# Sums by destination over spans of 64 nodes for 128 in a two-layer graph network

## The chip, the cores and the metric

One core of one Trainium2 chip runs the whole network. The metric is device time in microseconds, from start to end of one execution. Lower is better.

## The reference

There are 6250 nodes with 128 features (`x`), 206250 edges sorted by destination (`dst`), each with a source (`src`), a weight and 128 attributes. Both layers sum over edges:

```python
edge_index = jnp.stack([src, dst]); edge_index_t = jnp.stack([src, dst], axis=1)
h = jnp.maximum(_layernorm(x), 0.0)
# layer 0: (row, col) = (src, dst), with a loop of weight 1 at each node
deg = segment_sum(w, row); dinv = rsqrt(deg)
x = x + relu(segment_sum((dinv[row] * w * dinv[col])[:, None] * (h @ kernel)[col], row) + bias)
h = jnp.maximum(_layernorm(x), 0.0)
# layer 1: heads = src, tails = dst, E = edge attributes
msg_fwd  = concatenate([h[heads], E]) @ W_fwd + b_fwd
msg_back = concatenate([h[tails], E]) @ W_back + b_back
agg = segment_sum(concatenate([msg_fwd, msg_back]), concatenate([tails, heads])) / (cnt + 1e-7)
x = x + layernorm(leaky_relu(agg) + h) * gamma + beta
```

The weights are applied after the sums, since both are linear. So what has to be summed are rows of `g = dinv * h` by source, and edge attributes by source and by destination.

## The kernel before

**Groups.** The edges are cut into 202 groups of 1024 (8 for each of 128 partitions, `J = 8`). Since they are sorted by destination, a group touches few neighbouring nodes. `base_i[g]` holds the first destination of group `g`, and an edge's offset is its destination less that. The setup (`setup_and_degrees`) writes the offsets to DRAM (`dst_offset`), keeps them in the group's record (`rec`), and checks that every offset lies within the span that the sums by destination can hold (L449 to L453). If one does not, the flag `dense` is 0 and a general path with a scatter for every row runs in place of `first_layer` and `dense_sums`.

**What is done with a group.** Both stages that the change touches go through groups in the same way.
- VectorE compares the keys of the sources (L851, L1709; eight a group, each 128 x 128) to find edges of one source; TensorE multiplies with the result, so that each source's sum stands in one row (L966 and L967, or L1814).
- ScalarE copies those sums out of PSUM (L1039, L1895), and GpSimd adds them to tables in DRAM with indirect transfers, called scatters here, eight a group (L813, L1643).
- `spot_sums` (VectorE, L827 and L1687) compares the offsets of the 1024 edges with 0 to 127. The result, `sum_hot`, is 128 x 8 x 128. TensorE multiplies the attributes with it into one bank, `win_bank` (L962, L1812; eight products a group, the first three together at chunk 2), and `add_window` (L836, L1696) adds the 128 columns to `attr_sums` at `base`.
- In the first layer only: the rows of `g` that belong to the destinations are loaded (`window`, 128 rows from `base`, L791), the offsets are loaded to all partitions (`rel_b`, L783) and compared with each partition's number (L856, `spread_hot`), and TensorE spreads the rows to the edges (L949). ScalarE weighs them (L1032, `pay`).

**The stages.** `first_layer` takes groups 0 to 107, beside products for the other part of the graph (13 pairs of node tiles, L988, L998). `dense_sums` takes the other 94, most of them in steps beside the 25 tiles of a dense product by counts of edges (L1743, L1744, L1794, L1850, L1870), the last 88 in the first 22 tiles, four a tile.

**Order.** Every engine has a fixed program, and semaphores tie them. At a group's start VectorE runs, in this order, `spot_sums` of this group (after all products of the last), `add_window` of the last group, and then `prepare` for the next group with its eight L851 or L1709, with L856 behind the third. TensorE needs both of the first two at chunk 2:

```python
if j == 2:
    at_least(pe, window_added, g)
    pe.wait_ge(sum_ready, g + 1)
for jj in (range(3) if j == 2 else range(j, j + 1) if j > 2 else ()):
    nc.tensor.matmul(win_bank[:, 0:P], attrs[:, h, jj, :], sum_hot[:, jj, :], start=(jj == 0), stop=(jj == J - 1))
```

A scatter waits for ScalarE's copy and for the landing of the last scatter into its table; ScalarE's copy waits for the landing of the scatter that read its buffer before. SyncE loads in the order offsets, keys, record (after `sum_ready`, L785 and L1581), rows of `g`, attributes (after TensorE's products).

## Time and profile before

| | before |
|---|---|
| median of 3 runs | 4395.79 us (4393.73 to 4401.21) |
| the profiled execution | 4403.89 us |
| its span | 4402.1 us |
| TensorE, weight loads | 3390.4 us, 2833.3 us |
| VectorE | 3169.3 us |
| ScalarE | 1843.2 us |
| GpSimd | 3040.5 us |
| scatters of the first layer (L813) | 493 to 2235 us, 864 of them |
| scatters of the second stage (L1643) | 2444 to 4087 us, 752 of them |

Names in rows: PE is TensorE's matmuls, PEld its weight loads, DVE VectorE, ACT ScalarE, POOL GpSimd, SPq SyncE's queue. A row of a group of instructions reads: line, engine, operation, output<-inputs, shapes, count | busy us, mean ns of one | idle us of the engine just before them, and what ended that. Tiles of the first layer begin with `fl_`, those of the second stage with `ds_`; `shared` is a memory that several tiles of the second stage use, among them `same`, `sum_hot` and the sums. An fp32 matmul is two records.

### The profile page before, as it was taken

The page shows a single profiled execution, that of the slowest core. Times are in us where ns is not written, and L with a number is a line of the kernel's source. Part 1 is how long each engine was busy: PE and PEld are TensorE (multiplying, and loading weights), DVE is VectorE, ACT ScalarE, POOL GpSimd, SP SyncE. Part 2 cuts the span into 40 slices and gives each one's busy share as a digit, 9 for nine tenths or more (in the row PEclk, how much of TensorE's full clock was granted, in tenths as well). Part 3 has the DMA queues.
Part 4 walks back from the last instruction along what each step waited for, and adds up shares of the span by engine and source line. Part 5 has one row for each costly group of instructions (what it writes and reads, how often), then busy time and mean ns, then how long its engine had stood idle before and what let it go on. Part 6 is the DMA issues. An engine that isn't in the chain of part 4 may idle for free. (4 is left out here: it accounts for less than half of the span.)

```text
span 4402.1 us, 100368 instructions
## 1 busy us (share of the span) xinstructions
PE 3390.4 (77%) x30529; PEld 2833.3 (64%) x30529; DVE 3169.3 (72%) x8051; ACT 1843.2 (42%) x4498; POOL 3040.5 (69%) x1812
## 2 busy tenths in 40 slices
PE   1454599888889888889803499889888898889945
PEld 1344587777777777777703377767767677777635
DVE  6999888888888888878614776666666666666427
ACT  1021355545555555555404144444444444444513
POOL 2666488888888888888820688778777777777210
PEclk9989899999999999999956599999999999999977
DMA  9991587777777777777786555455445555554861
GB/s 162 279 217 16 128 142 140 139 140 135 135 141 139 141 136 135 137 135 141 129 131 120 105 84 85 75 78 82 77 77 78 84 77 80 77 83 72 97 124 30
DMA packets 682054, 504.19 MB, mean 115 GB/s; under 512 B 308854, under 2 KB 593920, under 8 KB 679754
## 3 DMA queue, kind: packets, MB, share of 16 engines
q0 software_dynamic: 260032, 176.60, 36.6%
q1 hardware_dynamic: 421475, 320.75, 29.9%
q8 instruction: 288, 4.72, 0.4%
q14 instruction: 259, 2.12, 0.2%
HBM read 283.43 MB, written 240.12 MB: 119 GB/s over the span
## 5 line engine op out<-in xcount | busy, mean ns | idle before, releaser
L1643 POOL DMA_INDIRECT gcn_sums<-shared,ds_to_i x752 | 1309.1, 1741 | 542.5 <-ACT shared L1895 327.6
L813 POOL DMA_INDIRECT gcn_sums<-fl_sums,fl_to_i x864 | 1459.3, 1689 | 290.9 <-DMA gcn_sums<-fl_sums,fl_to_i 151.9
L1850 PE MATMUL bank<-ds_counts,ds_parts 128*128 128x256 bf16 x3675 | 605.5, 278 | 0.0
L1039 ACT COPY fl_sums<-bank 128x256 f32<-128x256 f32 x864 | 324.7, 376 | 641.8 <-DMA gcn_sums<-fl_sums,fl_to_i 303.6
L1919 ACT COPY ds_turned<-bank 128x1024 bf16<-128x1024 bf16 (+1 forms) x325 | 313.1, 963 | 613.4 <-PE bank L1835 520.7
L1883 ACT CAST ds_counts<-bank 128x392 bf16<-128x392 f32 x800 | 382.9, 490 | 225.9 <-PE bank L1794 206.4
L1870 PE MATMUL bank<-ds_turned,ds_now 128*128 128x512 bf16 (+1 forms) x1950 | 463.7, 375 | 0.0
L851 DVE SCALAR_TENSOR_TENSOR fl_same<-fl_key_b,fl_pat,from_me 128x128 f32<-128x128 bf16 x864 | 375.5, 447 | 117.0 <-PE bank L967 93.1
L1779 DVE TENSOR_TENSOR src_sums<-src_sums,bank 128x512 f32<-128x512 f32 (+1 forms) x325 | 213.2, 656 | 278.8 <-PE bank L1870 274.2
L966 PE MATMUL bank<-fl_pay,fl_same 128*128 128x128 f32 x1728 | 350.9, 285 | 66.7 <-issue 38.1
L1812 PE MATMUL bank<-shared 128*128 128x128 f32 x1504 | 306.8, 308 | 115.1 <-DVE attr_sums L1696 87.1
L1709 DVE SCALAR_TENSOR_TENSOR shared<-shared,ds_pat,from_me 128x128 f32<-128x128 bf16 x752 | 312.3, 443 | 106.7 <-PE bank L1814 91.8
L962 PEld LDWEIGHTS bank<-fl_sum_hot,fl_attrs 128*128 128x128 f32 x1728 | 263.8, 192 | 183.4 <-issue 114.0
L1814 PE MATMUL bank<-shared 128*128 128x128 f32 x1504 | 319.2, 296 | 72.6 <-DMA shared<-in_edge_attr 48.7
L962 PE MATMUL bank<-fl_sum_hot,fl_attrs 128*128 128x128 f32 x1728 | 324.1, 290 | 56.0 <-DVE attr_sums L836 54.5
L1850 PEld LDWEIGHTS bank<-ds_counts,ds_parts 128*128 128x128 bf16 x3675 | 344.2, 100 | 32.6
L966 PEld LDWEIGHTS bank<-fl_pay,fl_same 128*128 128x128 f32 x1728 | 272.6, 195 | 113.9 <-issue 99.7
L998 PE MATMUL bank<-fl_hi_w,fl_lo_hot 128*128 128x98 bf16 x4992 | 289.1, 208 | 67.5 <-DVE fl_hi_w L890 61.6
L967 PE MATMUL bank<-fl_attrs,fl_same 128*128 128x128 f32 x1728 | 339.7, 279 | 0.0
L988 PE MATMUL bank<-fl_turned,fl_g_tile 128*128 128x512 f32 (+1 forms) x676 | 332.8, 574 | 3.6 <-DVE gcn_t L899 1.0
L585 PE MATMUL bank<-col_w,row_hot 128*128 128x200 bf16 x1616 | 174.1, 266 | 194.0 <-DVE col_w L507 188.5
L890 DVE TENSOR_TENSOR fl_hi_w<-fl_hi_hot,fl_twos 128x784 bf16<-128x784 bf16 x624 | 317.2, 565 | 8.7
(254 smaller groups left out, 7101.6 us busy)
## 6 DMA issues: line engine op xcount, KB each, us to landing
fl_attrs<-in_edge_attr SPq DMA_DIRECT2D x108, 512.0 KB
shared<-in_edge_attr SPq DMA_DIRECT2D x186, 256.0 KB
fl_rel_b<-dst_offset SPq DMA_DIRECT2D x108, 256.0 KB
fl_key_b<-src_key SPq DMA_DIRECT2D x108, 256.0 KB
gcn_sums<-zeros SPq DMA_DIRECT2D x40, 640.0 KB
shared<-src_key SPq DMA_DIRECT2D x94, 256.0 KB
gcn_sums<-fl_sums,fl_to_i POOLq DMA_INDIRECT x864
near<-src_float SPq DMA_DIRECT2D x1, 12892.0 KB
```

What stands on the lines that cost most here:

```text
L813: nc.gpsimd.indirect_dma_start(out=d.tab_gcn[j % K], out_offset=bass.IndirectOffsetOnAxis(ap=to_i[:, (GPI * kk + gi) % 4, j:j + 1], axis=0 ...
L851: nc.vector.scalar_tensor_tensor(same[:, j, :], key_p[:, h, :, j], pat_f[:, j:j + 1], d.from_me[:], ALU.is_equal, ALU.mult, accum_out=late ...
L962: nc.tensor.matmul(win_bank[:, 0:P], attrs[:, h, jj, :], sum_hot[:, jj, :], start=(jj == 0), stop=(jj == J - 1))
L966: nc.tensor.matmul(sum_bank[j % 2][:, 0:F], same[:, j, :], pay[:, j // U, j % U, :], start=True, stop=True)
L967: nc.tensor.matmul(sum_bank[j % 2][:, F:2 * F], same[:, j, :], attrs[:, h, j, :], start=True, stop=True).then_inc(summed, 1)
L988: nc.tensor.matmul(prod_bank[:, 0:n], g_tile[:, old, :], turned[:, (old + b) % 2, 0:n], start=True, stop=True).then_inc(prod_ready, 1)
L1039: nc.scalar.copy(sums[:, h, j, :], sum_bank[j % 2][:, 0:2 * F]).then_inc(staged, 1)
L1643: nc.gpsimd.indirect_dma_start(out=d.tab_gcn[j % K].rearrange("n (two f) -> (n two) f", two=2), out_offset=bass.IndirectOffsetOnAxis(ap=to ...
L1814: nc.tensor.matmul(sum_bank[:, j % U * F:(j % U + 1) * F], same[:, j, :], attrs[:, half, j % U, :], start=True, stop=True).then_inc(chunk_ ...
L1850: ins = nc.tensor.matmul(row_bank[:, 0:2 * P], parts[:, tile, s, :], counts[:, h, tile, :, :].rearrange("p b q -> p (b q)"), start=(tile = ...
L1870: ins = nc.tensor.matmul(back_bank[v][:, 0:n], now[:, h, half, s, :], turned[:, v, half, 0:n], start=(half == 0 and s == 0), stop=(half == ...
L1883: nc.scalar.copy(to, pair_bank[batch % B][:, 0:PB * HH].rearrange("p (c k) -> p k c", c=PB)).then_inc(pair_copied, 1)
```

## The change

The span falls from 128 to 64 nodes wherever destinations are summed or spread. `W = 64` is new. The setup's bound goes to 64, so a group with an offset of 64 or more would send the whole execution to the general path.

```diff
+W = 64
...
-                nc.vector.tensor_scalar(wide[:, 0:1], wide[:, 0:1], P - 0.5, None, ALU.is_gt)
+                nc.vector.tensor_scalar(wide[:, 0:1], wide[:, 0:1], W - 0.5, None, ALU.is_gt)
...
-        rel_b = sb("rel_b", [P, 2, P, J], BF16)
-        window = sb("window", [P, 2, F])
+        rel_b = sb("rel_b", [W, 2, P, J], BF16)
+        window = sb("window", [W, 2, F])
...
-        spread_hot = sb("spread_hot", [P, J, P])
+        spread_hot = sb("spread_hot", [W, J, P])
...
-        sum_hot = sb("sum_hot", [P, J, P])
+        sum_hot = sb("sum_hot", [P, J, W])
...
-                    sp.dma_start(flat(rel_b[:, h, :, :]), everywhere(d.dst_offset, g)).then_inc(rel_in[h], 16)
+                    sp.dma_start(flat(rel_b[:, h, :, :]), everywhere(d.dst_offset, g, W)).then_inc(rel_in[h], 16)
...
-                    sp.dma_start(window[:, h, :], d.g[bass.ds(base, P), :]).then_inc(window_in[h], 16)
+                    sp.dma_start(window[:, h, :], d.g[bass.ds(base, W), :]).then_inc(window_in[h], 16)
...
-                nc.vector.tensor_tensor(sum_hot[:], d.iota[:].unsqueeze(1).to_broadcast([P, J, P]), rec[:, h, 2, :].unsqueeze(2).to_broadcast([P, J, P]),
+                nc.vector.tensor_tensor(sum_hot[:], d.iota[:, 0:W].unsqueeze(1).to_broadcast([P, J, W]), rec[:, h, 2, :].unsqueeze(2).to_broadcast([P, J, W]),
                                         ALU.is_equal).then_inc(sum_ready, 1)
...
-                at = bass.ds(base, P)
-                nc.vector.tensor_tensor(d.attr_sums[:, at], d.attr_sums[:, at], win_bank[:, 0:P], ALU.add).then_inc(window_added, 1)
+                at = bass.ds(base, W)
+                nc.vector.tensor_tensor(d.attr_sums[:, at], d.attr_sums[:, at], win_bank[:, 0:W], ALU.add).then_inc(window_added, 1)
...
-                    nc.vector.tensor_scalar(spread_hot[:], rel_b[:, h, :, :].rearrange("p q j -> p j q"), d.part[:, 0:1], None,
+                    nc.vector.tensor_scalar(spread_hot[:], rel_b[:, h, :, :].rearrange("p q j -> p j q"), d.part[0:W, 0:1], None,
...
-                    nc.tensor.matmul(win_bank[:, 0:P], attrs[:, h, jj, :], sum_hot[:, jj, :], start=(jj == 0), stop=(jj == J - 1))
+                    nc.tensor.matmul(win_bank[:, 0:W], attrs[:, h, jj, :], sum_hot[:, jj, :], start=(jj == 0), stop=(jj == J - 1))
```

The second stage (`dense_sums`) gets the same edits in `sum_hot`, `spot_sums`, `add_window` and the product at L1812. It has no `rel_b` and no `window`.

## Rows read from the trace of the kernel before

**Rows 1.** The page, busy time of engines over the span.
```profile
PE 3390.4 (77%) x30529; PEld 2833.3 (64%) x30529; DVE 3169.3 (72%) x8051; ACT 1843.2 (42%) x4498; POOL 3040.5 (69%) x1812
```
**Rows 2.** Busy time in two stretches: PE, PEld, DVE, ACT, POOL (instructions), PE clock, DMA share, GB/s.
```profile
1000.00:1200.00 200.00, 174.74 (x1599) 150.53 (x1598) 164.60 (x468) 101.80 (x287) 167.74 (x99) 0.98 0.78 139
3200.00:3400.00 200.00, 174.34 (x1580) 138.28 (x1577) 128.14 (x343) 86.12 (x150) 154.32 (x89) 0.94 0.50 77
```
**Rows 3.** Groups by line on GpSimd, 600 to 2150 us and 2605 to 3940 us.
```profile
L813 POOL DMA_INDIRECT gcn_sums<-fl_sums,fl_to_i x767 | 1299.9, 1695 | 252.5 <-DMA gcn_sums<-fl_sums,fl_to_i 133.7 <-issue 104.3 <-ACT fl_sums L1039 14.5
...
L1643 POOL DMA_INDIRECT gcn_sums<-shared,ds_to_i x612 | 1060.9, 1733 | 276.1 <-issue 157.8 <-ACT shared L1895 105.8 <-DMA gcn_sums<-shared,ds_to_i 12.5
```
**Rows 4.** The page, groups of the scatters over the span.
```profile
L1643 POOL DMA_INDIRECT gcn_sums<-shared,ds_to_i x752 | 1309.1, 1741 | 542.5 <-ACT shared L1895 327.6
L813 POOL DMA_INDIRECT gcn_sums<-fl_sums,fl_to_i x864 | 1459.3, 1689 | 290.9 <-DMA gcn_sums<-fl_sums,fl_to_i 151.9
```
**Rows 5.** The lines of the scatters: duration in ns min/median/max, first and last start.
```profile
L813 POOL DMA_INDIRECT gcn_sums<-fl_sums,fl_to_i x864: 1557/1561/2632, 493.0 to 2233.8; - x173
...
L1643 POOL DMA_INDIRECT gcn_sums<-shared,ds_to_i x752: 1557/1561/2819, 2443.6 to 4085.4; - x188
```
**Rows 6.** Timeline about 1004 us, VectorE and GpSimd: start us, us, instruction.
```profile
1003.90 1.16 DVE L856 TENSOR_SCALAR fl_spread_hot<-fl_rel_b,part 128x1024 f32<-128x1024 bf16 x1
...
1004.09 2.41 POOL L813 DMA_INDIRECT gcn_sums<-fl_sums,fl_to_i  x1 [0.30 <-issue]
```
**Rows 7.** Timelines: first and last held scatter beside L827, then beside L1687.
```profile
518.96 1.22 DVE L827 TENSOR_TENSOR fl_sum_hot<-iota,fl_rec 128x1024 f32<-128x1024 f32 x1
...
519.16 2.46 POOL L813 DMA_INDIRECT gcn_sums<-fl_sums,fl_to_i  x1 [0.30 <-DMA gcn_sums<-fl_sums,fl_to_i]
...
2146.10 1.23 DVE L827 TENSOR_TENSOR fl_sum_hot<-iota,fl_rec 128x1024 f32<-128x1024 f32 x1
...
2146.66 2.10 POOL L813 DMA_INDIRECT gcn_sums<-fl_sums,fl_to_i  x1 [0.30 <-DMA gcn_sums<-fl_sums,fl_to_i]
...
2479.66 1.22 DVE L1687 TENSOR_TENSOR shared<-iota,ds_rec 128x1024 f32<-128x1024 f32 x1
...
2480.60 1.72 POOL L1643 DMA_INDIRECT gcn_sums<-shared,ds_to_i  x1 [0.30 <-issue]
...
4062.71 1.22 DVE L1687 TENSOR_TENSOR shared<-iota,ds_rec 128x1024 f32<-128x1024 f32 x1
...
4063.64 1.72 POOL L1643 DMA_INDIRECT gcn_sums<-shared,ds_to_i  x1 [0.30 <-issue]
```
**Rows 8.** Groups by line and form on VectorE, over the span.
```profile
L827 DVE TENSOR_TENSOR fl_sum_hot<-iota,fl_rec 128x1024 f32<-128x1024 f32 x108 | 131.7, 1220 | 57.0 <-issue 42.1 <-PE bank L967 12.2 <-DVE fl_to_i L864 2.4
...
L1696 DVE TENSOR_TENSOR attr_sums<-attr_sums,bank 128x128 f32 x94 | 26.4, 281 | 0.4 <-issue 0.4
...
L1678 DVE TENSOR_TENSOR src_sums<-src_sums,ds_parts 128x1280 f32<-128x1280 f32 x5 | 7.5, 1493 | 0.2
```
**Rows 9.** Timelines of a tile's start, 2934 to 2946 us: VectorE, TensorE, GpSimd.
```profile
2934.49 1.23 DVE L1743 TENSOR_TENSOR ds_lo_hot<-ds_numbers,ds_twos 128x2048 bf16<-128x2048 bf16 x1
...
2937.66 0.28 DVE L1696 TENSOR_TENSOR attr_sums<-attr_sums,bank 128x128 f32 x1
...
2937.99 0.94 PE L1812 MATMUL bank<-shared 128*128 128x128 f32 x6 [2.39 <-DVE attr_sums L1696]
2938.76 0.39 PE L1814 MATMUL bank<-shared 128*128 128x128 f32 x2
...
2945.03 1.56 POOL L1643 DMA_INDIRECT gcn_sums<-shared,ds_to_i  x1 [2.13 <-ACT shared L1895]
```
**Rows 10.** Waits of TensorE, 600 to 2150 and 2605 to 3940 us: total us, times, longest.
```profile
PE bank L962 <- DVE attr_sums L836: 50.6, 84, 2.0
...
PE bank L1812 <- DVE attr_sums L1696: 46.8, 23, 2.6
```
**Rows 11.** Timeline of TensorE about 279 us: fp32 matmuls with few moving columns.
```profile
278.97 0.42 PE L555 MATMUL bank<-start,ahead 128*128 128x50 f32 x2 [0.62 <-DVE start L423]
279.23 0.39 PE L556 MATMUL bank<-start,wrap 128*128 128x49 f32 x2
```

More of the change, by code:

```diff
@@ L1811, in sum_chunk @@
                 for jj in (range(3) if j == 2 else range(j, j + 1) if j > 2 else ()):
[L1812 removed]
+                    nc.tensor.matmul(win_bank[:, 0:W], attrs[:, jj // U, jj % U, :], sum_hot[:, jj, :], start=(jj == 0), stop=(jj == J - 1))
                 pe.wait_ge(same_ready, ch + 1)
```

13 lines of the change are left out of this document (6 added, 7 removed).

## The prediction

> **What bounds the kernel now.** Read the page first, for which engines are full: TensorE is busy for 77% of the span, GpSimd for 69%, and no engine is full by that figure [rows 1]. The share is an average, so the stretches come next. Two of 200 us, one in each stage that the change touches, show GpSimd at 168 and 154 us with 99 and 89 instructions, TensorE at about 174 us in both, VectorE at 165 and 128 us [rows 2]. GpSimd only issues scatters there, and its busy time leaves out what passes between two of them. The groups by line give that: in 600 to 2150 us 767 scatters take 1299.9 us with 252.5 us idle before them, or 0.33 us each; in 2605 to 3940 us 612 take 1060.9 with 276.1 idle [rows 3]. Before nearly every scatter the idle time is 0.30 us, which is the least that shows anywhere and so the cost of going from one to the next. 1299.9 + 252.5 is 1552 of 1550 us: **in the first layer GpSimd is never without work**. There 767 x 0.305 = 234 of the idle us is that floor, and 18.6 us is a wait for something. In the second stage it is 276.1 - 612 x 0.305 = 89 us, nearly all of it for ScalarE's copy of the sums (105.8 us with its floors): GpSimd sets the pace between hiccups, and TensorE causes those.
>
> The last thing to see is a scatter's own time. The median is 1.561 us in both stages, the mean 1.689 and 1.741, the longest 2.6 and 2.8 [rows 4, 5]. So (1.689 - 1.561) x 864 = 111 us and (1.741 - 1.561) x 752 = 135 us are spent in scatters that are longer than the rest. Where that comes from shows when the timelines of GpSimd and VectorE are laid side by side: a scatter that starts during a long VectorE instruction ends 1.43 us after **that instruction's** end. The one at 1004.09 lasts 2.41 us, to 1006.50; VectorE's comparison for the spread (L856) ran from 1003.90 to 1005.06 [rows 6]. The comparison for the sums (L827, L1687) does the same: 518.96 + 1.22 = 520.18, and the scatter of 519.16 ends at 521.62, 1.44 later; 2479.66 + 1.22 = 2480.88, and that of 2480.60 ends at 2482.32, 1.44 later [rows 7]. A scatter so held costs what is left of VectorE's instruction less 0.13 us. Additions that read PSUM (L899, L1779, L836) hold none in the timeline.
>
> **The change, part by part.**
>
> The comparison for the sums goes from 1024 to 512 elements per partition. VectorE's one with both inputs in SBUF takes 1.220 us for 1024 and 1.493 us for 1280, which is 1.07 ns an element [rows 8]; 512 fewer take 0.546 us off, and leave **0.674 us**. Over 108 + 94 groups that is 110 us of VectorE, which by itself is worth nothing: VectorE has 35 and 72 of 200 us free [rows 2]. It counts in two ways.
>
> *Holds.* If a scatter's start falls anywhere, an instruction of length L holds on average (L - 0.13)^2 / 2T, with T the spacing of scatters, 2.02 us in the first layer and 2.2 in the second stage (200 us by 99 and 89 [rows 2]). Before: 1.09^2 / 4.04 = 0.29 us a group, after: 0.544^2 / 4.04 = 0.073; times 108 is 24 us gained. In the second stage 1.19 / 4.4 - 0.296 / 4.4 = 0.203, times 94 is 19 us. Together 43 us. The other way is to count. I find 32 held scatters at L827, 19.7 us in all, and 71 at L1687, 39.3 us in all (first and last of each in [rows 7]); with each hold shortened by 0.546 us and the starts as they are, 4.3 and 10.8 us stay, which gains 15 + 28.5 = 44 us. Both ways agree in the sum and I take **43 us**. All of it is on the path in the first layer, and in the second stage wherever GpSimd sets the pace. Bounds: nothing (the holds pass on to the next instruction), and 59 us (all of them gone).
>
> *The wait at a tile's start.* Once per tile of the second stage TensorE waits 2.4 us for the addition of the last window (L1696), which stands on VectorE behind three long comparisons: L1743 from 2934.49, L1744, L1687, and the addition at 2937.66; TensorE goes on at 2937.99, and GpSimd then stands idle for 2.13 us before 2945.03 [rows 9]. In that window there are 23 such waits, 46.8 us [rows 10]. The chain gets 0.55 us shorter by L1687 and 0.07 us by the addition (0.281 us for 128 columns, 1.06 ns each by the same slope [rows 8]). Over 21 tiles that is **13 us**; from 0, if the idle time is filled from elsewhere, to 2 x 13 where a tile has a second such gap. In the first layer the same wait is 0.6 us once a group (84 of them, 50.6 us [rows 10]), and it goes altogether, but GpSimd has work all the while: nothing.
>
> *The window's products* (L962, L1812) get 64 moving columns for 128. I cost this at **nothing**, and this is the choice that matters most on TensorE. Each fp32 product is two records, and each loads 128 x 128 weights. The only fp32 products with few moving columns are at 278.97 us: two of 50 and two of 49 columns. The pairs last 0.42 and 0.39 us, as long as a pair with 128 columns (0.39, at 2938.76 [rows 9]), and the second pair starts 0.26 us behind the first, so one record takes some 0.11 to 0.13 us whatever it moves [rows 11]. The weight load sets that. At most, if a record went with its columns, 16 records a group gain 0.054 us each, 0.86 us a group (rival below).
>
> *The spread* (L856, L949) works on 64 partitions for 128. Elements per partition and moving columns stay as they are, so 1.16 us [rows 6] and the records stay too: nothing. But it moves: it stands behind L827 and L836 on VectorE with nothing that would stop it, so it runs 0.62 us earlier against the scatters. In 48 of 108 groups a scatter starts some 0.2 us into L856 and is held, 38.5 us in all (one in [rows 6]). With 0.62 us more lead the hold is 0.3 us for 0.9: up to 26 us gained if all 48 keep their place, or as much lost if other scatters now start there. I take 0.
>
> *Loads.* The row offsets are 128 KB for 256 and the rows of g 32 KB for 64, in 108 groups. No engine waits for either in the list of waits. They share the DMA engines with the scatters, whose landing GpSimd sometimes waits for: of the 18.6 us above, so 0 to 19 us; I take 0. SyncE issues as many transfers in the same order. The records of edges (L1583) wait for the comparison's end and go out up to 0.55 us earlier, but SyncE mostly stands at an earlier wait, for TensorE; VectorE may then wait 0.5 us longer for them, off GpSimd's path. The bound in the setup is a constant, and no added instruction or wait stands anywhere in the change.
>
> Sum: 43 + 13 = **56 us**. The profiled execution took 4403.9 us (its span is 4402.1); it would take 4348. The median of the runs is 4395.8, 8 us less, and I forecast **4340 us**. About 0.2%, or 9 us, is what a measurement of this kernel can tell from no change (its three runs lie within 7.5 us).
>
> **The rivals.**
> 1. *The holds stay.* The scatter waits for whatever VectorE does next, or GpSimd's time moves to its idle share. For it: VectorE is 80% busy in the first layer and one long comparison follows the other. Against it: the additions from PSUM and the short ones behind L827 and L1687 hold nothing. Left is the tile's wait: 4396 - 13 = 4383 us, and 4396 if that goes too. The Trainium skill (SBUF — State Buffer, "Who interferes with whom") has both rules: a VectorE instruction with two SBUF inputs contends with a GpSimd one that reads SBUF, and such an instruction leaves descriptor writing alone, since that needs the write interface. By the second the comparisons of sums would hold no scatter at all, and this rival would be the case; the trace speaks against that, with the scatters of 2.46 and 1.72 us beside L827 and L1687.
> 2. *TensorE gains too.* 0.86 us a group is 3.4 us a tile, against some 4.6 us a tile that GpSimd stands idle (89 us in 19.5 tiles). In 22 tiles at most 75 us more: 4265 us. The Trainium skill (TensorE: Matmul & The Clock Gate, "Back-to-back issue gap") gives an isolated product a gap that falls with its moving columns, which would speak for it; its "LDWEIGHTS" section has the load depend on the 128 columns of weights. The pairs of 49 and 50 columns decide for the load.
> 3. *Slower: the spread's comparison meets a scatter in every group.* VectorE's work keeps its place against the scatters, since all wait for their landings. If the 0.62 us puts a scatter's start right behind L856's, each of 108 groups is held by up to 1.16 - 0.13 = 1.03 us, 111 us for 38.5 now: +73 us, which less 56 is 17 us slower, 4413 us. It decides from a total hold at L856 of 38.5 + 56 = 95 us, 0.88 a group. For it: 48 of 108 already lie at nearly one phase. Against it: they lie at its front now, and moving it earlier takes it off them.
> 4. *The change doesn't do what it says:* a group spans over 64 nodes and the general path runs. 206250 edges on 6250 nodes are 33 a node, so 1024 edges span 31 nodes; 64 is twice that.
>
> **How the numbers follow.** The forecast 0.61 (its own range 4310 to 4375: below it all holds gone and two waits a tile, 59 + 26 us; above it half of the holds and no tile's wait); the first rival 0.20, half of it at 4383 and half at no change; TensorE gains 0.06; slower 0.12; the general path 0.01. The range is 4300 to 4390: it takes in the forecast and most of the first rival. Faster by over 0.2%: 0.61 + 0.06 + 0.10 = 0.77. Within: 0.10 and a little of the third, 0.11. Slower: 0.12.
>
> **What would show it.** L827 and L1687 at 0.67 us; a mean scatter of 1.66 to 1.68 us in the first layer and 1.69 to 1.71 in the second stage, at an unchanged median; the wait for L836 gone and that for L1696 at 1.8 us; the pair of records at L1812 still at 0.39 us; L856 at 1.16 to 1.2 us. It is wrong if the scatters' mean stays (first rival), if TensorE's records at L1812 get closer (second), or if L856 holds more than 0.88 us a group (third).

## The result, and the profile after

The changed kernel takes 4422.2 us (median of four runs, 4418.9 to 4426.7) where the kernel before takes 4394.8 beside it: a ratio of 1.0062, with a 95% interval of 1.0046 to 1.0078. It is slower by 27 us; the forecast was 4340 us, faster by 56. Every line of the code stands one further down than before (L813 is L814, L856 is L857). The span grew from 4402.1 to 4422.1 us.

The page of the changed kernel, its engines and the two groups of scatters that answer to [rows 1, 4]:

```profile
PE 3482.2 (79%) x30313; PEld 2902.2 (66%) x30529; DVE 3068.0 (69%) x8051; ACT 1835.4 (42%) x4498; POOL 3071.2 (69%) x1812
...
L814 POOL DMA_INDIRECT gcn_sums<-fl_sums,fl_to_i x864 | 1537.8, 1780 | 276.4 <-DMA gcn_sums<-fl_sums,fl_to_i 128.8
L1644 POOL DMA_INDIRECT gcn_sums<-shared,ds_to_i x752 | 1260.9, 1677 | 553.9 <-ACT shared L1896 337.0
```

The two lines of scatters of the changed kernel by source, minimum, median and maximum in ns, then first and last start in us (beside [rows 5]):

```profile
L814 POOL DMA_INDIRECT gcn_sums<-fl_sums,fl_to_i x864: 1557/1566/4513, 485.0 to 2289.8; - x173
...
L1644 POOL DMA_INDIRECT gcn_sums<-shared,ds_to_i x752: 1557/1561/2812, 2495.7 to 4104.7; - x188
```

The two stages went opposite ways. The second, from its first scatter's start to its last one's end, took 1643.4 us before and takes 1610.5: 33 gained, and the mean scatter fell from 1741 to 1677 ns. The first layer took 1742.3 and takes 1806.4: 64 lost, and its mean scatter rose from 1689 to 1780 ns, 864 x 0.091 = 79 us. Its median stayed at 1.57; its longest went from 2.6 to 4.5. Counted one by one, no scatter of the first layer was over 2.65 us before; now 63 are, and what they last over 1.56 us each is 94 us in all. The two stages give +31 us; 4 us less between them, 8 us less ahead of the first layer and 1 us more at the end leave the 20 us of the two spans.

VectorE's groups of the changed kernel by line and form, beside [rows 6, 8]:

```profile
L857 DVE TENSOR_SCALAR fl_spread_hot<-fl_rel_b,part 64x1024 f32<-64x1024 bf16 x108 | 125.4, 1161 | 0.0
...
L828 DVE TENSOR_TENSOR fl_sum_hot<-iota,fl_rec 128x512 f32<-128x512 f32 x108 | 74.1, 686 | 40.4 <-PE bank L968 18.2 <-issue 17.0 <-DVE fl_to_i L865 5.1
...
L1697 DVE TENSOR_TENSOR attr_sums<-attr_sums,bank 128x64 f32 x94 | 20.7, 220 | 11.4 <-issue 8.1 <-PE bank L1815 2.3
```

The comparison of sums takes 0.686 us (0.674 forecast), the spread's 1.16 as forecast. The scatters held beside the sums' comparison fell as the second way of counting had it: at L828 from 19.7 us to 4.1 (forecast 4.3), at L1688 from 39.3 to 5.0 (forecast 10.8).

**Where the long scatters come from.** The same piece of VectorE's work in both kernels, with a scatter that starts when as much of it is left. Timelines of the kernel before, VectorE and GpSimd (start us, duration us, instruction):

```profile
1005.56 0.56 DVE L884 TENSOR_TENSOR fl_hi_hot<-fl_numbers,fl_twos 128x784 bf16<-128x784 bf16 x1
1006.04 0.69 DVE L885 TENSOR_TENSOR fl_lo_hot<-fl_numbers,fl_twos 128x1024 bf16<-128x1024 bf16 x1
1006.64 0.45 DVE L851 SCALAR_TENSOR_TENSOR fl_same<-fl_key_b,fl_pat,from_me 128x128 f32<-128x128 bf16 x1
...
1007.01 1.52 DVE L890 TENSOR_TENSOR fl_hi_w<-fl_hi_hot,fl_twos 128x784 bf16<-128x784 bf16 x3
...
1006.80 1.67 POOL L813 DMA_INDIRECT gcn_sums<-fl_sums,fl_to_i  x1 [0.30 <-DMA gcn_sums<-fl_sums,fl_to_i]
```

And of the changed kernel:

```profile
819.24 1.15 DVE L857 TENSOR_SCALAR fl_spread_hot<-fl_rel_b,part 64x1024 f32<-64x1024 bf16 x1
820.31 0.67 DVE L900 TENSOR_TENSOR gcn_t<-gcn_t,bank 128x512 f32<-128x512 f32 x1
820.91 0.55 DVE L885 TENSOR_TENSOR fl_hi_hot<-fl_numbers,fl_twos 128x784 bf16<-128x784 bf16 x1
821.38 0.68 DVE L886 TENSOR_TENSOR fl_lo_hot<-fl_numbers,fl_twos 128x1024 bf16<-128x1024 bf16 x1
821.98 0.43 DVE L852 SCALAR_TENSOR_TENSOR fl_same<-fl_key_b,fl_pat,from_me 128x128 f32<-128x128 bf16 x1
...
822.35 1.51 DVE L891 TENSOR_TENSOR fl_hi_w<-fl_hi_hot,fl_twos 128x784 bf16<-128x784 bf16 x3
...
822.14 3.20 POOL L814 DMA_INDIRECT gcn_sums<-fl_sums,fl_to_i  x1 [0.30 <-DMA gcn_sums<-fl_sums,fl_to_i]
```

Before, the scatter starts with 0.29 us of L851 left and is held by that instruction alone: 1006.64 + 0.45 = 1007.09, and it ends at 1008.47, 1.38 later. The three multiplications behind it (L890) don't matter. After, with 0.27 us of L852 left, it is held through all three of L891: they end at 823.86, the scatter at 825.34, 1.48 later. Before, all 32 scatters that meet the row in this place last 1.65 to 1.69 us. After, 34 of 41 last over 2.65. VectorE's instructions have the same durations, so the row didn't get slower. What differs ahead of it is the spread's comparison, on 64 partitions for 128.

### The profile page after: what moved, and what is told of

Same layout as the page of the kernel before. It is cut to its first block and busy times, and to the rows that moved or that the text cites. A ratio compares the mean times of both kernels' runs of the same rounds, so it can differ in the third digit from the quotient of the medians.

```text
span 4422.1 us, 100152 instructions
## 1 busy us (share of the span) xinstructions
PE 3482.2 (79%) x30313; PEld 2902.2 (66%) x30529; DVE 3068.0 (69%) x8051; ACT 1835.4 (42%) x4498; POOL 3071.2 (69%) x1812
## 5 line engine op out<-in xcount | busy, mean ns | idle before, releaser
L814 POOL DMA_INDIRECT gcn_sums<-fl_sums,fl_to_i x864 | 1537.8, 1780 | 276.4 <-DMA gcn_sums<-fl_sums,fl_to_i 128.8
L1644 POOL DMA_INDIRECT gcn_sums<-shared,ds_to_i x752 | 1260.9, 1677 | 553.9 <-ACT shared L1896 337.0
L852 DVE SCALAR_TENSOR_TENSOR fl_same<-fl_key_b,fl_pat,from_me 128x128 f32<-128x128 bf16 x864 | 373.1, 442 | 240.2 <-PE bank L968 222.9
L967 PE MATMUL bank<-fl_pay,fl_same 128*128 128x128 f32 x1728 | 400.9, 315 | 95.9 <-ACT fl_sums L1040 82.2
L1871 PE MATMUL bank<-ds_turned,ds_now 128*128 128x512 bf16 (+1 forms) x1734 | 417.4, 370 | 11.6 <-issue 0.4
L1815 PE MATMUL bank<-shared 128*128 128x128 f32 x1504 | 353.1, 318 | 71.9 <-DVE shared L1710 49.3
L963 PEld LDWEIGHTS bank<-fl_sum_hot,fl_attrs 128*128 128x128 f32 x1728 | 277.9, 202 | 124.2 <-issue 114.9
L968 PE MATMUL bank<-fl_attrs,fl_same 128*128 128x128 f32 x1728 | 352.5, 288 | 0.0
L1813 PE MATMUL bank<-shared 128*128 128x64 f32 x1504 | 274.8, 287 | 96.5 <-DVE attr_sums L1697 69.2
L999 PE MATMUL bank<-fl_hi_w,fl_lo_hot 128*128 128x98 bf16 x4992 | 302.9, 213 | 33.9 <-DVE fl_hi_w L891 33.8
L891 DVE TENSOR_TENSOR fl_hi_w<-fl_hi_hot,fl_twos 128x784 bf16<-128x784 bf16 x624 | 315.5, 559 | 8.7
L999 PEld LDWEIGHTS bank<-fl_hi_w,fl_lo_hot 128*128 128x128 bf16 x4992 | 260.1, 101 | 69.4 <-issue 43.9
```

The costliest lines, as they stand in the source:

```text
L814: nc.gpsimd.indirect_dma_start(out=d.tab_gcn[j % K], out_offset=bass.IndirectOffsetOnAxis(ap=to_i[:, (GPI * kk + gi) % 4, j:j + 1], axis=0 ...
L852: nc.vector.scalar_tensor_tensor(same[:, j, :], key_p[:, h, :, j], pat_f[:, j:j + 1], d.from_me[:], ALU.is_equal, ALU.mult, accum_out=late ...
L967: nc.tensor.matmul(sum_bank[j % 2][:, 0:F], same[:, j, :], pay[:, j // U, j % U, :], start=True, stop=True)
L968: nc.tensor.matmul(sum_bank[j % 2][:, F:2 * F], same[:, j, :], attrs[:, h, j, :], start=True, stop=True).then_inc(summed, 1)
L999: last = nc.tensor.matmul(pair_bank[at][:, c * HH:(c + 1) * HH], lo_hot[:, go % 2, q, :], hi_w[:, go % 2, m, q, :], start=(m == 0), stop=( ...
L1644: nc.gpsimd.indirect_dma_start(out=d.tab_gcn[j % K].rearrange("n (two f) -> (n two) f", two=2), out_offset=bass.IndirectOffsetOnAxis(ap=to ...
```

## The experiments

In the edits one constant stands for each part: W1 is the columns of the first layer's window sums, H1 those of its comparison, R1 the partitions of row offsets, rows of g, spread comparison and spread product, W2 the second stage's columns. The changed kernel has 64 in all, the kernel before 128. "First layer" and "mean" are read from each kernel's profiled execution; "long" counts the first layer's scatters of over 2.65 us, a bound just above the longest of the kernel before (2.63). In the edits `...` stands for lines left out.

| kernel | ratio, 95% interval | first layer us | mean ns | long |
|---|---|---|---|---|
| before | 1 | 1742 | 1689 | 0 |
| changed | 1.0062 [1.0046, 1.0078] | 1806 | 1780 | 63 |
| e1 second stage only | 0.9910 [0.9896, 0.9924] | 1745 | 1692 | 1 |
| e2 rows on 128 | 0.9913 [0.9899, 0.9928] | 1739 | 1687 | 2 |
| e3 comparison of 1024 | 0.9966 [0.9955, 0.9977] | 1774 | 1736 | 16 |
| e4 delay | 0.9980 [0.9971, 0.9990] | 1765 | 1729 | 14 |
| e5 loads on 64, work on 128 | 0.9885 [0.9870, 0.9900] | 1719 | 1680 | 0 |
| e6 loads on 128, spread on 64 | 1.0119 [1.0104, 1.0135] | 1824 | 1782 | 55 |
| e7 rows apart | 0.9964 [0.9952, 0.9976] | 1747 | 1691 | 0 |
| e8 only the product on 64 | 0.9903 [0.9888, 0.9918] | 1735 | 1687 | 0 |
| e9 copy behind | 1.0144 [1.0123, 1.0164] | 1830 | 1807 | 62 |
| e10 small instruction on 64 | 1.0300 [1.0280, 1.0320] | 1868 | 1840 | 75 |
| e11 the same on 128 | 1.0051 [1.0035, 1.0067] | 1754 | 1703 | 4 |
| e12 spread on 96 | 1.0073 [1.0057, 1.0089] | 1812 | 1782 | 60 |
| e13 own wait | 0.9867 [0.9840, 0.9893] | 1705 | 1665 | 0 |
| e14 e10 with a wait | 1.0020 [1.0005, 1.0034] | 1749 | 1699 | 0 |
| e15 small copy on 64 | 1.0125 [1.0101, 1.0149] | 1781 | 1735 | 25 |
| e16 small one, second stage | 1.0306 [1.0286, 1.0327] | 1746 | 1693 | 1 |
| e17 e2 with the wait | 0.9851 [0.9836, 0.9866] | 1710 | 1660 | 0 |
| e18 e5 with the wait | 0.9832 [0.9818, 0.9845] | 1701 | 1662 | 0 |

### Which part of the change costs

```diff
-W = 64
+W1, H1, R1, W2 = 128, 128, 128, 64
```

> The span of 64 in the second stage alone; the first layer as before. Theory A (the loss is the first layer's: VectorE runs 0.6 us earlier against the scatters, and scatters now start in front of unbroken rows of VectorE instructions; the second stage gained what was forecast): the second stage, first scatter to last, falls from 1643 us to about 1611, the first layer stays at 1742 with no scatter over 2.65 us; in all 33 us faster than before, ratio 0.992 to 0.993. Rival B (the two stages' changes work on each other, or the loss lies outside the scatters): no faster than before, ratio 0.998 or more.

```diff
-W = 64
+W1, H1, R1, W2 = 64, 64, 128, 64
```

> The changed kernel, but offsets, rows of g and the spread's comparison of the first layer stay at 128 partitions. Theory A (VectorE's timing): the loss stays, ratio 1.004 to 1.008, 90 or so us in scatters over 2.65 us. Rival C (loads onto 64 partitions, or a spread with 64 rows, disturb the first layer): the loss goes, ratio about 0.988 to 0.993, since the second stage keeps its gain of 33 us.

e1 gives 0.9910: the second stage's part is worth 0.9%, and the first layer stays as it was. e2 gives 0.9913: with the spread back on 128 partitions the first layer's narrower sums cost nothing and bring 4 us at most. The whole loss, 1.0062 - 0.9913 = 1.5% or 65 us, hangs on offsets, rows of g and spread at 64 partitions, which the forecast costed at nothing. So theory A, the mere timing of VectorE's work, fails: it had e2 at 1.004 to 1.008.

### Only the order of events?

```diff
-W = 64
+W1, H1, R1, W2 = 64, 128, 64, 64
```

> The changed kernel, but the first layer's comparison for the sums keeps its 1024 elements (the product and the addition use 64 of the 128 columns). Theory A: VectorE is only 0.07 us earlier than before, so the first layer goes back to about 1742 us from 1806, and with the second stage's gain of 33 us the ratio is 0.990 to 0.994. Rival C (loads or the spread on 64 partitions): the loss stays, 1.004 or more. By the forecast's sum this kernel would be 15 to 24 us slower than the changed one.

```diff
                 at_least(dve, summed, J * (g + 1))
+                nc.vector.tensor_tensor(idle[:], win_bank[:, 0:W1].unsqueeze(1).to_broadcast([P, DELAY, W1]), d.iota[:, 0:W1].unsqueeze(1).to_broadcast([P, DELAY, W1]), ALU.add)
```

> The changed kernel with one more VectorE instruction a group in the first layer, ahead of the addition of the window: an addition of 448 elements that reads PSUM and writes a spare tile, about 0.62 us, which puts everything behind it back to its place before the change. Theory A: more work, and yet faster than the changed kernel: the first layer near 1742 us or under it by the 15 us that the shorter comparison holds less; ratio to before 0.986 to 0.994. Rival D (VectorE's short comparison itself brings the loss, by whatever way other than its timing, or VectorE is simply the bound): no better than the changed kernel, or up to 40 us slower than it, ratio 1.006 to 1.015.

e3 puts the 1024-element comparison back and lengthens the path to the spread by 0.53 us; e4 does so with an addition that reads PSUM (448 elements, DELAY = 7). Both cut the long scatters from 63 to 16 and 14 and give 0.9966 and 0.9980. So where the scatters meet the row has a say, but neither comes to the 0.9913 of e2: something stays that order alone doesn't explain. Theory A had both at 0.994 or less.

### Load, comparison or product?

```diff
-        rel_b = sb("rel_b", [W, 2, P, J], BF16)
+        rel_b = sb("rel_b", [P, 2, P, J], BF16)
...
-                    sp.dma_start(flat(rel_b[:, h, :, :]), everywhere(d.dst_offset, g, W)).then_inc(rel_in[h], 16)
+                    sp.dma_start(flat(rel_b[0:R1, h, :, :]), everywhere(d.dst_offset, g, R1)).then_inc(rel_in[h], 16)
...
-                    nc.vector.tensor_scalar(spread_hot[:], rel_b[:, h, :, :].rearrange("p q j -> p j q"), d.part[0:W, 0:1], None,
+                    nc.vector.tensor_scalar(spread_hot[:], rel_b[:, h, :, :].rearrange("p q j -> p j q"), d.part[:, 0:1], None,
...
+            nc.vector.memset(rel_b[R1:P, :, :, :], -1.0).then_inc(numbers_ready, 1)
+            nc.vector.memset(window[R1:P, :, :], 0.0).then_inc(numbers_ready, 1)
```

> The changed kernel, with offsets and rows of g still loaded for 64, but compared and multiplied on all 128 partitions (the upper 64 are set once, to an offset that never matches and to zeros). Theory C1 (the loads onto 64 partitions bring the loss): slow as the changed kernel, first layer 1790 us or more, ratio 1.004 or more. Theory C2 (the spread with 64 rows brings it): fast as the kernel with all three at 128, first layer near 1739 us, ratio 0.990 to 0.993, and TensorE under 90 us at half clock between 480 and 2190 us.

```diff
-                    sp.dma_start(flat(rel_b[:, h, :, :]), everywhere(d.dst_offset, g, W)).then_inc(rel_in[h], 16)
+                    sp.dma_start(flat(rel_b[:, h, :, :]), everywhere(d.dst_offset, g, P)).then_inc(rel_in[h], 16)
...
-                    nc.vector.tensor_scalar(spread_hot[:], rel_b[:, h, :, :].rearrange("p q j -> p j q"), d.part[0:W, 0:1], None,
+                    nc.vector.tensor_scalar(spread_hot[:], rel_b[0:R1, h, :, :].rearrange("p q j -> p j q"), d.part[0:R1, 0:1], None,
...
-                    last = nc.tensor.matmul(row_bank[:, q * F:(q + 1) * F], spread_hot[:, half * U + q, :], window[:, h, :], start=True, stop=True)
+                    last = nc.tensor.matmul(row_bank[:, q * F:(q + 1) * F], spread_hot[0:R1, half * U + q, :], window[0:R1, h, :], start=True, stop=True)
```

> The reverse: offsets and rows of g loaded for 128, compared and multiplied on 64 partitions. Theory C1 (loads): fast, first layer near 1739 us, ratio 0.990 to 0.993. Theory C2 (the spread with 64 rows: TensorE's granted clock falls to half for 190 us of the first layer in the changed kernel, 54 before): slow, first layer 1775 us or more, ratio 0.999 or more, 150 us or more at half clock. If both this and the one before are fast, or both slow, neither is the cause and any small shift of time can bring the loss (theory A in a wider form).

In both edits R1 is 64, and the rows of g are loaded like the offsets. e8 is e6 with the comparison on 128 partitions again, so that TensorE's product alone takes 64 rows.

> Offsets and rows of g loaded for 128 and compared on 128 partitions; only TensorE's product of the spread takes 64 rows of both. Theory C2 in its narrow form (64 rows lower TensorE's clock, which shifts the work against the scatters): slow, first layer 1775 us or more, ratio 0.999 or more, 150 us or more at half clock. Otherwise fast, first layer near 1739 us, ratio 0.990 to 0.993.

The three runs single out one instruction. Loads on 64 partitions with work on 128 (e5) are the fastest of these, 0.9885, with no long scatter; the product on 64 rows (e8) does nothing, 0.9903 for 0.9913; VectorE's comparison on 64 partitions with full loads (e6) gives 1.0119 and 55 long scatters. e6 and e8 differ in that comparison alone, and lie 2.2% or 95 us apart. In the place shown above, 0 of e8's 23 scatters and 0 of e2's 23 are long.

### Breaking the rows

```diff
+                dve.wait_ge(hi_ready, GOES * tile + go + 1)
                 nc.vector.tensor_tensor(in_twos(lo_hot[:, go % 2, :, :]), counted_to(P), per_pair(hh, 0, go, P), ALU.is_equal)
...
                     last = nc.vector.tensor_tensor(in_twos(hi_w[:, go % 2, m, :, :]), in_twos(hi_hot[:]), per_pair(hh, 2 + m, go, HH), ALU.mult)
+                    if m < 2:
+                        last.then_inc(weighed, 1)
+                        dve.wait_ge(weighed, 2 * (GOES * tile + go) + m + 1)
```

> The changed kernel with VectorE's unbroken rows in the first layer taken apart: it waits for the end of the comparison L885 before L886, and for each of the first two weighings L891 before the next. Theory A (a scatter that meets such a row is held to the row's end, up to 1.7 us): no or few scatters over 2.65 us (63 in the changed kernel, 94 us beyond 1.56 us each), the first layer at 1760 us or less from 1806, though VectorE does the same work with waits between; ratio under 0.997. Rival D (the rows are not what holds them, or VectorE is the bound): scatters over 2.65 us remain, no faster than the changed kernel, 1.005 or more.

With a wait between the two comparisons of a row and between its three multiplications, no scatter is long, and the ratio is 0.9964: better than the changed kernel, short of e2.

### Is it a state?

```diff
                                             ALU.is_equal).then_inc(spread_ready, 1)
+                    nc.vector.tensor_copy(mark[:], d.part[:, 0:4])
```

> The changed kernel with one more instruction: right behind VectorE's comparison of the spread (64 partitions, 1.15 us) stands a copy of four elements on all 128 partitions into a tile of its own. Theory S: an instruction of VectorE on 64 partitions leaves something behind, so that the row of instructions after it holds a scatter of GpSimd from end to end, until one on 128 partitions that copies comes (the two copies of the comparison's keys lifted it in every trace so far). Expected by S: no scatter of the first layer over 2.65 us (63 in the changed kernel), first layer near 1740 us, ratio to the kernel before 0.989 to 0.993. Theory P: only the phase matters, in which the scatters meet the row; the copy lengthens the row by some 0.07 us, 94 x 0.07 = 7 us: long scatters stay, ratio 1.002 to 1.009.

The next two add one instruction of four elements to the kernel **before**, where every other instruction has 128 partitions:

```diff
                                             ALU.is_equal).then_inc(spread_ready, 1)
+                    nc.vector.tensor_scalar(mark[0:64, :], d.iota[0:64, 0:4], d.part[0:64, 0:1], None, ALU.is_equal)
```

> The kernel before (spans of 128 everywhere) with one more instruction: behind the spread's comparison stands a comparison of four elements on 64 partitions with a scalar per partition, into a tile of its own. Theory S, if any instruction on 64 partitions leaves the state: scatters of over 2.65 us appear in the first layer (none in the kernel before) and its mean scatter goes from 1689 to 1730 ns or more: ratio 1.005 to 1.02. Theory L, a variant of S: it takes the long comparison on 64 partitions itself, and a short one leaves nothing: ratio 1.000 to 1.003, no long scatter. Theory P (phase alone): as L.

e11 writes `mark[:]` from `d.iota[:, 0:4]` and `d.part[:, 0:1]` instead.

> The control of the run with four elements on 64 partitions: the kernel before with the same small comparison on 128 partitions. Every theory: ratio 0.999 to 1.003 (94 x 0.07 us = 7 us at most), no scatter over 2.65 us in the first layer. If this one shows long scatters too, the count of partitions is not what makes them, and an instruction that shifts the row is.

```diff
-W = 64
+W1, H1, R1, W2 = 64, 64, 96, 64
```

> The changed kernel with row offsets, rows of g and the spread's comparison and product on 96 partitions in place of 64; spans of 64 in the sums stay. Theory S, if any count under 128 leaves the state: long scatters stay, ratio 1.002 to 1.009 as for 64 partitions. If it takes a count of 64 (or under 65), or if it is only the phase and the load's 0.16 us longer issue that do it: no long scatters, ratio 0.989 to 0.993 as with 128 partitions (0.9913).

e9 refutes one half of the theory as it stood: a copy on all partitions lifts nothing (62 long, and with 1.0144 slower than either theory had it). e10 against e11 bears out the other half, and is the clearest pair of the study: the two kernels differ in how many partitions one instruction of four elements covers, and take 1.0300 and 1.0051. The direction is the theory's, the sizes are not: it had e10 at 1.005 to 1.02 and e11 at 0.999 to 1.003 with no long scatter, and e11 has four. Pages of e10 and then of e11:

```profile
L815 POOL DMA_INDIRECT gcn_sums<-fl_sums,fl_to_i x864 | 1589.4, 1840 | 286.8 <-issue 140.5
```

```profile
L815 POOL DMA_INDIRECT gcn_sums<-fl_sums,fl_to_i x864 | 1471.6, 1703 | 289.8 <-DMA gcn_sums<-fl_sums,fl_to_i 150.2
```

The same place in both. Timelines of e10, VectorE and GpSimd:

```profile
1106.00 0.23 DVE L860 TENSOR_SCALAR fl_mark<-iota,part 64x4 f32<-64x4 f32 x1
...
1107.81 0.44 DVE L853 SCALAR_TENSOR_TENSOR fl_same<-fl_key_b,fl_pat,from_me 128x128 f32<-128x128 bf16 x1
...
1108.18 1.51 DVE L893 TENSOR_TENSOR fl_hi_w<-fl_hi_hot,fl_twos 128x784 bf16<-128x784 bf16 x3
...
1109.97 0.69 DVE L902 TENSOR_TENSOR gcn_t<-gcn_t,bank 128x512 f32<-128x512 f32 x1
...
1107.84 3.59 POOL L815 DMA_INDIRECT gcn_sums<-fl_sums,fl_to_i  x1 [0.30 <-DMA gcn_sums<-fl_sums,fl_to_i]
```

And of e11:

```profile
823.70 0.22 DVE L860 TENSOR_SCALAR fl_mark<-iota,part 128x4 f32<-128x4 f32 x1
...
825.51 0.43 DVE L853 SCALAR_TENSOR_TENSOR fl_same<-fl_key_b,fl_pat,from_me 128x128 f32<-128x128 bf16 x1
...
825.55 1.56 POOL L815 DMA_INDIRECT gcn_sums<-fl_sums,fl_to_i  x1 [0.30 <-issue]
```

In e10 the scatter starts 0.03 us into L853 and ends at 1111.43, 1.46 us after the addition from PSUM (L902) has taken over; in e11 it starts 0.04 us into the same instruction and isn't held at all. Of the scatters that start in the first 0.06 us of such an L853, in a row without a pause behind the small instruction, 21 of 22 are long in e10 and none of 16 in e11. e12 adds that 96 partitions do it as 64 do (1.0073, 60 long), so it takes a count below 128, not half.

**The long scatters of e11.** A row can hold a scatter to its end without a narrow instruction too. In the kernel before, 30 scatters start in the first L890 of a row that has run without a pause since the spread's comparison, and 3 of them end 1.43 us after the third L890. One of the three:

```profile
2093.35 1.55 DVE L890 TENSOR_TENSOR fl_hi_w<-fl_hi_hot,fl_twos 128x784 bf16<-128x784 bf16 x3
...
2093.70 2.63 POOL L813 DMA_INDIRECT gcn_sums<-fl_sums,fl_to_i  x1 [0.30 <-issue]
```

They last 2.62 to 2.63 us, and the bound of 2.65 leaves them out. In the same place 5 of e11's 42 are held to the third multiplication's end or beyond, its four long ones among them, and all 37 of e10's. So the narrow instruction makes a rule of what is otherwise an exception; it doesn't bring something that never happens without it.

**TensorE's clock,** which the expectations of e5, e6 and e8 name, isn't what does it. Over the first layer the granted clock is 0.98 in the kernel before and 0.93 in the changed one, but it is 0.96 in both e8 and e10, whose ratios are 0.9903 and 1.0300. The first layer of e8 and then of e10 (us; busy time of PE, PEld, DVE, ACT, POOL; clock, DMA share, GB/s):

```profile
486.20:2221.60 1735.40, 1581.59 (x13838) 1345.35 (x13836) 1356.85 (x3994) 906.08 (x2476) 1457.50 (x864) 0.96 0.78 137
```

```profile
483.40:2351.70 1868.30, 1574.62 (x13837) 1345.75 (x13835) 1429.66 (x4102) 858.29 (x2476) 1589.41 (x864) 0.96 0.73 127
```

**What ends it.** In the changed kernel, e9, e10 and e12 there are 260 long scatters in the first layer. I looked for the last narrow instruction ahead of each, and for pauses of VectorE in between. All 260 lie in a row that runs without a pause of over 30 ns from that instruction on, and none behind a pause. (The 55 of e6 and 16 of e3 do the same.) Other scatters meet the same row behind a pause: in the changed kernel 22 start in the last L852 ahead of the three L891 with at least 0.1 us of it left and a longer pause since the spread's comparison, and none is long, where 34 of the 41 without a pause are. What the copies of the keys, named in e9's expectation, had seemed to lift, the pause behind them had. That makes a forecast that can fail:

```diff
                                             ALU.is_equal).then_inc(spread_ready, 1)
+                    dve.wait_ge(spread_ready, g + 1)
```

> The changed kernel as it is, with one wait: behind the spread's comparison on 64 partitions VectorE waits for that comparison's own semaphore, so that it pauses for a moment. In the profiled executions of the changed kernel, of those with 96 partitions, with the copy behind and with four elements on 64 partitions all 260 scatters of over 2.65 us lie in a row of VectorE instructions that runs without a pause (over 30 ns) from the narrow instruction on, and none lies behind a pause. Theory S with that addition (the state ends at VectorE's next pause): no scatter over 2.65 us, first layer within 10 us of the 1738.6 us with 128 partitions, ratio 0.989 to 0.993. Rival: the narrow count only shifts when the scatters meet the row, or the state ends elsewhere (at the pause the row happens to have): the long scatters stay, ratio 1.002 to 1.009.

```diff
-                    nc.vector.tensor_scalar(mark[0:64, :], d.iota[0:64, 0:4], d.part[0:64, 0:1], None, ALU.is_equal)
+                    nc.vector.tensor_scalar(mark[0:64, :], d.iota[0:64, 0:4], d.part[0:64, 0:1], None, ALU.is_equal).then_inc(marked, 1)
+                    dve.wait_ge(marked, g + 1)
```

> The kernel before with the comparison of four elements on 64 partitions behind the spread's comparison (ratio 1.030 without the wait), and VectorE waiting for the small comparison's own semaphore. The pause ends the state: no scatter over 2.65 us, ratio 1.000 to 1.008 (as 1.0051 for four elements on 128 partitions, and the wait's own pause of some 0.1 us, 94 times). The state outlasts a pause: ratio 1.02 to 1.035.

The long scatters go in both, as the state has it. The changed kernel with its own wait takes 0.9867 of before, faster than the 0.989 to 0.993 that the state's end alone should give (see e17); e10 falls from 1.0300 to 1.0020. The wait also moves the scatters against the row, so the place has to be compared too: in e10 all 37 scatters that start in the first L893 of an unbroken row are long; in e14 7 start at the same multiplication behind the pause, with as much of it left (0.3 to 0.5 us), and the longest lasts 1.91 us. Timeline of e13, VectorE, the comparison and what follows (in brackets the pause):

```profile
1010.43 1.14 DVE L857 TENSOR_SCALAR fl_spread_hot<-fl_rel_b,part 64x1024 f32<-64x1024 bf16 x1
1011.79 0.69 DVE L901 TENSOR_TENSOR gcn_t<-gcn_t,bank 128x512 f32<-128x512 f32 x1 [0.21 <-DVE fl_spread_hot L857]
```

The pause is 0.19 to 0.23 us in most groups and 0.03 at the least; 13 scatters of e13 start in the row behind a pause of 0.03 to 0.06 us, and none is long. (The profiled execution of e13 reaches its first scatter at 562.0 us, 77 us later than the changed kernel's; it is read by stage alone.)

### How general is it?

```diff
-                    nc.vector.tensor_scalar(mark[0:64, :], d.iota[0:64, 0:4], d.part[0:64, 0:1], None, ALU.is_equal)
+                    nc.vector.tensor_copy(mark[0:64, :], d.iota[0:64, 0:4])
```

> The kernel before with a copy of four elements on 64 partitions in the place of the comparison of four elements. If any VectorE instruction on fewer than 128 partitions leaves the state: long scatters as with the comparison (77 of over 2.65 us), ratio 1.02 to 1.035. If it takes an instruction with a scalar per partition (as both the spread's and the small comparison have): no long scatters, ratio 1.000 to 1.007.

```diff
+                nc.vector.tensor_scalar(mark[0:64, go % GOES, :], d.iota[0:64, 0:4], d.part[0:64, 0:1], None, ALU.is_equal)
                 nc.vector.tensor_tensor(in_twos(lo_hot[:, go % 2, :, :]), counted(P), per_place(0, P), ALU.is_equal)
```

> The kernel before with the comparison of four elements on 64 partitions in the second stage instead, ahead of each pair of one-hot comparisons (L1743, L1744), and none in the first layer. If the state is no peculiarity of the first layer: scatters that meet the first of the pair are held to the end of the second, the second stage's mean scatter goes from 1741 ns to 1780 or more and the stage from 1643 us to 1670 or more, ratio 1.006 or more, first layer as before. If the state needs the first layer's row (three multiplications behind two comparisons): ratio 0.999 to 1.004.

e15 lies between its two theories: 1.0125, with 25 long scatters, of which 20 start in the first L893 of a row and last to the third's end. At that instruction 27 of e15's 32 scatters in an unbroken row are held to the third's end or beyond, for 3 of 30 before and all 37 of e10; in the place of e10's and e11's rows above it has no long one among 32. So a narrow copy leaves less than a narrow instruction with a scalar per partition, and whether part of its loss is only the order of events stays open. (The expectation speaks of 77 long ones in e10; there are 75.)

e16 shows the same in the other stage. Its page, then timelines of VectorE and GpSimd:

```profile
L1645 POOL DMA_INDIRECT gcn_sums<-shared,ds_to_i x752 | 1547.1, 2057 | 440.7 <-ACT shared L1898 217.0
```

```profile
3005.03 0.27 DVE L1745 TENSOR_SCALAR ds_mark<-iota,part 64x4 f32<-64x4 f32 x1 [0.26 <-PE bank L1797]
3005.17 1.21 DVE L1746 TENSOR_TENSOR ds_lo_hot<-ds_numbers,ds_twos 128x2048 bf16<-128x2048 bf16 x1
3006.30 0.96 DVE L1747 TENSOR_TENSOR ds_hi_hot<-ds_numbers,ds_twos 128x1568 bf16<-128x1568 bf16 x1
...
3005.64 3.38 POOL L1645 DMA_INDIRECT gcn_sums<-shared,ds_to_i  x1 [0.30 <-issue]
```

The scatter starts in L1746 and is held through L1747 and beyond (3007.26 + 1.76 = 3009.02). The stage's mean scatter is 2057 ns for 1741 and the stage 1784 us for 1643, while the first layer stays at 1746. The ratio, 1.0306, is well above the 1.006 that the expectation asks for. (This profiled execution reaches its first scatter at 581.0 us, 88 us later than the kernel before; the stage alone is read.)

### Is the pause worth something by itself?

```diff
-W1, H1, R1, W2 = 64, 64, 64, 64
+W1, H1, R1, W2 = 64, 64, 128, 64
...
                                             ALU.is_equal).then_inc(spread_ready, 1)
+                    dve.wait_ge(spread_ready, g + 1)
```

> The control of the changed kernel with its own wait (0.9867): offsets, rows of g and the spread on 128 partitions again (0.9913 without a wait), and the same wait behind the spread's comparison. If what the wait gives back is the state of the narrow instruction alone, it does nothing here, where no instruction is narrow: first layer 1730 to 1745 us, ratio 0.990 to 0.993. If the pause also serves the scatters by itself (one that waits for a row's end comes through in it), the first layer is at 1705 to 1720 us and the ratio 0.984 to 0.989, as with 64 partitions and the wait.

> The version with 64-partition loads and 128-partition work (0.9885) with the same wait added. If the pause serves by itself and adds to the narrow loads: ratio 0.982 to 0.987. If the wait only ends the state: 0.987 to 0.990. More than 0.991: the pause costs its own length 94 times over (0.2 us each, 19 us) once there is no state to end.

It is. Where no instruction is narrow, the wait takes 0.9913 to 0.9851, 27 us, and the first layer from 1739 to 1710 us: here the theory that gave the wait nothing but the state's end was wrong. So if the pause is worth as much in the changed kernel, 0.62% of the 1.95% that the wait gives it is the pause's own and 1.3%, 58 us, the state's; that the two add up so is argued, not shown. The holds at the three multiplications fall from 22 us (e2) to 10 (e17); that the pause lets a scatter in earlier, or moves the row off the scatters, no run tells apart. e18, narrow loads, wide work and the wait, is the fastest kernel of the study: 4325.9 us, 0.9832 [0.9818, 0.9845], against 0.9885 for e5 without the wait.

## Why the prediction was wrong

**The step that failed** is that of the spread: "The spread (L856, L949) works on 64 partitions for 128. Elements per partition and moving columns stay as they are, so 1.16 us and the records stay too: nothing." The durations were right (1.161 us, and TensorE's product on 64 rows changes nothing, e8). The price was not: behind a narrow VectorE instruction the scatters are held through whole rows, 1.5% or 65 us by e2 against the changed kernel. That still counts what the narrower loads gain; with the loads alike the narrow comparison costs 78 us (the changed kernel against e5) or 95 us (e6 against e8). Forecast and measurement are 82 us apart, and this term is most of it. What makes a narrow instruction do this stays open.

**The holds' law was too simple.** "Ends 1.43 us after that instruction's end" holds for most scatters of before, but says nothing of the instruction behind. That a row can hold a scatter to its end was in the trace before, at 3 of 30 scatters of the first L890, the longest scatter of the layer (2.63 us) among them. The traces of before had only 128-partition instructions in these stages, so how often it happens behind a narrow one couldn't be seen there; a bound for "fewer partitions" should have been put on this edit, as long as a row (1.5 us and more), rather than only on its 0.62 us of lead.

**The holds at the sums, 43 us:** right in the second stage, where 34 us went at L1688 for 28.5 forecast; in the first layer 15.6 us went at L828 as forecast, but e2, without the state, is only 4 us faster there than the kernel before. The first rival (holds pass on to other instructions) was right for that stage.

**The wait at a tile's start, 13 us:** not found in GpSimd's time. Waits of TensorE in the changed kernel, 2605 to 3940 us (total, times, longest), beside [rows 10]:

```profile
PE bank L1813 <- DVE attr_sums L1697: 35.5, 19, 2.0
```

It is 1.87 us each, for 2.03 before, where 0.62 less was forecast. There are fewer of them, though: over the whole stage they go from 31 waits with 87.1 us in all to 27 with 69.2. None of the 18 us shows on GpSimd, whose waits for ScalarE's copy went from 327.6 to 337.0 us. The second stage's 33 us are the shorter scatters (48 us), less 15 us more idle time between them. So the part without the spread was worth 38 us (e2), not 56.

**The loads,** 0 taken of 0 to 19 us: too low. With narrow loads the timed runs are 8 us faster (e18 against e17, e5 against e8), 12 (e5 against e2) or 25 (the changed kernel against e6). In e5's first layer GpSimd's idle time is 13 us less than in e2's (275.7 for 288.7).

**TensorE's products, nothing:** right. Timeline of TensorE in the changed kernel, pairs of one chunk:

```profile
516.55 0.33 PE L963 MATMUL bank<-fl_sum_hot,fl_attrs 128*128 128x64 f32 x2
516.72 0.44 PE L967 MATMUL bank<-fl_pay,fl_same 128*128 128x128 f32 x2
516.99 0.39 PE L968 MATMUL bank<-fl_attrs,fl_same 128*128 128x128 f32 x2
```

The next pair starts 0.17 us behind the 64-column one, and the pair after it another 0.27 us later. Over 540 chunks the median starts of a 64-column pair's two records, and of the two records behind them, lie 58 + 112 + 165 = 335 ns apart where they lay 112 + 112 + 112 = 336. So a record with fewer columns does take less time itself, against what the prediction read from [rows 11], but the records behind it take that back.

**The third rival** had the sign, not the mechanism. It set 95 us of holds at the spread's comparison as the point from which it decides; scatters that start in L857 lose 48.5 us in all (38.5 before), and 12 of the 63 are held on through the L900 and L885 behind it. What decided was behind the comparison.

The Trainium skill (SBUF — State Buffer, "Who interferes with whom") has a VectorE instruction with at most one SBUF input, outside the two-port modes, leave GpSimd alone. By that rule the spread's comparison, which reads one tile and one scalar per partition, would hold no scatter. Here 62 of the 63 that start during L857 last over 1.6 us, and all 48 in the kernel before. At 1.13 ns an element (1.161 us for 1024) it shows no gain from a faster mode, so the measurement decides against the rule, unless the scalar counts as a second input; no run tells.

## What to carry to other kernels

An instruction on fewer partitions isn't free because it is as long. If GpSimd issues indirect transfers while VectorE works, look at the spread of those transfers' durations, not at their median, and compare them at the same phase. As far as this kernel shows, keep VectorE's operands on all 128 partitions (preset the unused ones and narrow only the loads), or let VectorE pause behind a narrow instruction, by a wait for its own semaphore.

## What the runs showed of the hardware

- Behind a VectorE instruction on 64 or 96 partitions with a scalar per partition, the instructions of an unbroken row mostly hold an indirect transfer's issue to the row's end (3.2 to 3.6 us in the places shown, for 1.56 to 1.79 without the narrow instruction). Four elements do it. A pause of VectorE of 0.03 to 0.2 us ends it, a 128-partition copy doesn't; a narrow copy has less of it. Without a narrow instruction it is rare (3 of 30 before, 5 of 42 in e11, for 37 of 37 in e10). What the state is inside the chip stays open, as does why 7 of the changed kernel's 41 scatters in that place escape it.
- SyncE needs longer to issue a load onto 64 partitions than onto 128. Its lines in e2 (128 partitions), then in the changed kernel (minimum, median and maximum in ns); in e12, with 96, the median is 338 as in e2:

```profile
L792 SPq DMA_DIRECT2D fl_window<-g x108: 333/338/352, 474.9 to 2169.0; - x108
```

```profile
L792 SPq DMA_DIRECT2D fl_window<-g x108: 482/493/524, 474.6 to 2236.3; - x108
```

It costs nothing that the runs show: e5 and e18 load onto 64 partitions and are the fastest without and with the wait.
